# Layer-norm and weight-sum stage of a transformer block: loads of x on another queue, three buffers, and work spread over three engines

## The chip, the cores and the metric

The kernel runs on 8 cores of one Trainium2 chip. Each core takes one of the 8 sequences and runs the same program on it. The metric is the device time of the slowest core in microseconds (us), as a median over runs. Engines: TensorE (PE in the profile), VectorE (DVE), ScalarE (ACT), GpSimd (POOL), and SyncE (SP), which here only issues transfers.

## The reference, cut to what matters

```python
x = x + attn(layernorm(x), Wq, Wk, Wv, Wo)      # x: 8 x 4096 x 1024, f32; one head, d_k = 128, causal
x = x + ffn(layernorm(x), w_gate, w_up, w_down)  # 1024 -> 4096 -> 1024

def layernorm(x):                    # no gain, no bias
    return (x - mean(x)) / sqrt(var(x) + 1e-5)

def weight_quant(w):                 # one scale for a whole matrix
    scale = 1.0 / clip(mean(abs(w)), 1e-5)
    return clip(round(w * scale), -1, 1) / scale
# ffn: down(silu(gate(x)) * up(x)); every matmul takes weight_quant(w) and activations rounded to 8 bits a row
```

The scale of a weight matrix needs the sum of |w| over all of it, so each of the three matrices (16 MB each in f32) is read once for its sum and once more to be quantized.

## The kernel before

A core's 4096 rows of x are 32 tiles of 128 rows (`NT`). The program is written down engine by engine: `sc.op(engine, fn, waits, inc)` appends an instruction to the list of one engine ('t' TensorE, 'v' VectorE, 's' ScalarE, 'g' GpSimd, 'q' SyncE), with the semaphore values that it waits for. Each engine runs its list strictly in the order in which the calls were made, its transfers among it. An instruction whose wait is not met holds all that stands behind it on its engine. There is no scheduler: the order of the Python calls is the order of the work.

The stages are:

1. **Phase 1** (lines 162 to 307): for each of 32 tiles, load x, compute mean and variance, normalize, transpose, and compute Q, K and V. Between the tiles the weight matrices are read in 96 pieces of 128x1024 f32 (512 KB) and the sum of |w| of each piece goes to a column of `wsums`.
2. `emit_scales` (L309): three small serial chains from `wsums` to the scales of the three matrices.
3. Attention in eight groups of four tiles, with the second read and quantization of the weights between them (`emit_w2_piece`, L355).
4. Output projection and first residual, gate and up matmuls, down matmul. These take most of the time, and the change does not touch them.

The change is in phases 1 and 2 of this list. The loop of phase 1 (L294 to L302) is, for tile i: `emit_p1_A(i + 1)`, `emit_p1_B(i)`, `emit_p1_geo(i)`, then three calls of `emit_w1_piece`.

- `emit_xload_p1` (L164) loads tile i of x into one of two buffers, `x_st[i % 2]`. GpSimd issues it (L169), after the normalization of tile i-2 has read the buffer.
- `emit_p1_A(i)` (L217): the sum of x on VectorE (L222), the sum of squares on ScalarE (L227, Square with an accumulator).
- `emit_p1_B(i)` (L230): mean, its square and the variance on VectorE (L235, L237, L239, each behind a drain), the square root on ScalarE (L242), the reciprocal and the bias on VectorE (L244, L247), and then the normalization on ScalarE (L249), which writes `ln1_sb`, the first quarter of `nqh_sb`. Below it is called Ident(i).
- `emit_p1_geo(i)` (L257): 8 transposes on TensorE (L262), their eviction on VectorE (L265), 24 matmuls for Q, K and V (L271, L275, L279), then the evictions of Q and V on VectorE (L282, L286) and of K on ScalarE (L284).
- `emit_w1_piece(idx)` (L189): SyncE loads a piece into one of four staging buffers (L194) once the sum that read that buffer four pieces ago is done; ScalarE sums |w| (L198, Abs with an accumulator). The four buffers are the halves of `wst2` (named wstage in the profile) and parts of `nqh_sb` and `nqt_sb`.

So in phase 1 GpSimd's list holds only x loads, and SyncE's only loads of weight pieces.

## Time and profile before

| what | us |
|---|---|
| median of 2 runs | 2716.04 (2715.21 to 2716.87) |
| the profiled execution, its own time | 2719.91 |
| its span, slowest core (core 6) | 2718.4 |
| spans of the 8 cores | 2704.9 to 2718.4 |
| phase 1 on core 6, start to the last sum of a weight piece | about 393 |

The profiled execution took 2719.9 us, 1.5 us more than the span between the first and the last instruction of its slowest core, and 3.9 us more than the median of the runs. A row of the timeline has the start and the duration in us, the engine, the line of the kernel, the operation, what it writes and reads, a count, and in brackets how long its engine stood idle before it and what ended that. "SPq" is a transfer issued by SyncE. In the table of transfers the last number is the time from issue to landing.

### The profile page before, as it was taken

To read this page: it belongs to the slowest core of one execution; us is meant where nothing else is said; L and a number is where in the kernel's file an instruction comes from. 1 tells how busy PE (TensorE), PEld (TensorE's weight loads), DVE (VectorE), ACT (ScalarE), POOL (GpSimd) and SP (SyncE) were. 2 spreads that over 40 slices of the span, in tenths; PEclk is the share of its full clock that TensorE was granted. 3 is DMA by queue.
4 is the path that set the end of the run, shared out by engine and by line. 5 is a ranking of instruction groups with operands and counts; after the bars stand their busy time and mean duration, and the time that the engine had idled before them with its cause. 6 is when DMAs were issued, how large, how long until landed. Compare 5 with 4: busy or idle time off the path is not lost.

```text
span 2718.4 us, 25524 instructions; the slowest of 8 cores (2704.9 to 2718.4 us)
## 1 busy us (share of the span) xinstructions
PE 1694.8 (62%) x9479; PEld 881.5 (32%) x9618; DVE 912.9 (34%) x1481; ACT 862.2 (32%) x893; POOL 50.1 (2%) x104
## 2 busy tenths in 40 slices
PE   1333331222212377778778778778778766999999
PEld 1222231222200133333334334334334333444444
...
GB/s 151 188 183 184 186 168 263 218 95 102 102 199 268 124 24 47 32 39 47 31 39 47 32 39 47 31 39 47 31 39 47 16 74 205 155 155 155 154 150 115
DMA packets 74603, 290.09 MB, mean 107 GB/s; under 512 B 10864, under 2 KB 12912, under 8 KB 62192
## 3 DMA queue, kind: packets, MB, share of 16 engines
...
## 4 chain that ended last, share of the span: by engine, by line
PE 57%; DVE 11%; ACT 11%; DMA 10%; issue 8%; DVEq 2%; POOL 1%; ACTq 0%; POOLq 0%; SPq 0%
PE pb L760 18%; PE pb L753 17%; PE pb L899 16%; DMA wdqh<-wdq_st 5%; DVE h_sb L772 3%; DMA x_st<-x 3%; ACT kres L770 3%; ACT nqh_sb L249 1%; DVE st_cols L777 1%; ACT wdq_st L380 1%; PE pb L464 1%; ACT ln_scr L227 1%; PE pb L439 1%; ACT wstage L198 1%; DVEq L369 1%
## 5 line engine op out<-in xcount | busy, mean ns | idle before, releaser
L753 PE MATMUL pb<-wgq,qres 128*128 128x512 bf16 x1952 | 772.5, 396 | 254.1 <-DVE qres L736 251.3
L760 PE MATMUL pb<-wuq,qres 128*128 128x512 bf16 x2048 | 807.8, 394 | 43.0 <-DVE h_sb L772 38.1
L899 PE MATMUL pb<-wdq_sb,nqt_in 128*128 128x512 bf16 x2007 | 442.2, 380 | 24.8 <-DMA nqt_in<-nqh 22.4
L772 DVE SCALAR_TENSOR_TENSOR h_sb<-pb,st_cols,kres 128x1024 f32<-128x1024 f32 x128 | 164.3, 1284 | 739.0 <-ACT kres L770 739.0
L753 PEld LDWEIGHTS pb<-wgq,qres 128*128 128x128 bf16 x2048 | 207.3, 101 | 552.0 <-issue 333.7
L770 ACT ACTIVATE kres<-pb,st_cols 128x1024 f32<-128x1024 f32 x128 | 142.7, 1115 | 497.3 <-PE pb L760 335.2
L760 PEld LDWEIGHTS pb<-wuq,qres 128*128 128x128 bf16 x2048 | 206.0, 101 | 254.3 <-issue 35.5
L899 PEld LDWEIGHTS pb<-wdq_sb,nqt_in 128*128 128x128 bf16 x2048 | 200.9, 98 | 265.9 <-issue 25.7
L464 PE MATMUL pb<-qres,kres 128*128 128x128 bf16 x528 | 51.1, 255 | 242.1 <-ACT pt L482 227.7
L830 ACT ACTIVATE nqh_sb<-h_sb,konst 128x4096 bf16<-128x4096 f32 x32 | 118.6, 3708 | 215.0 <-DVE h_sb L828 215.0
L262 PE MATMUL pb<-ident_sb,nqh_sb 128*128 128x128 bf16 x256 | 32.4, 307 | 239.8 <-ACT nqh_sb L249 239.8
L909 DVE SCALAR_TENSOR_TENSOR out_sb<-pb,c_all,x_in 128x512 f32<-128x512 f32 x32 | 24.0, 751 | 431.1 <-PE pb L899 431.1
L777 DVE TENSOR_REDUCE st_cols<-h_sb 128x1 f32<-128x1024 f32 x128 | 156.1, 1220 | 11.7
L464 PEld LDWEIGHTS pb<-qres,kres 128*128 128x128 bf16 x528 | 40.8, 116 | 247.8 <-issue 245.0
L262 PEld LDWEIGHTS pb<-ident_sb,nqh_sb 128*128 128x128 bf16 x256 | 24.8, 138 | 247.1 <-issue 247.1
L828 DVE TENSOR_SCALAR h_sb<-h_sb,st_cols,konst 128x4096 f32<-128x4096 f32 x32 | 77.2, 2411 | 5.6 <-DVE c_all L826 5.6
L702 ACT ACTIVATE qres<-ln_scr,konst 128x1024 bf16<-128x1024 f32 x32 | 36.7, 1147 | 130.4 <-DVE ln_scr L695 130.4
L609 PE MATMUL pb<-wo_sb,ot_sb 128*128 128x512 bf16 x30 | 18.2, 607 | 88.1 <-DVE ot_sb L571 85.3
L802 ACT ACTIVATE nqt_sb<-pb 128x2048 bf16<-128x2048 bf16 x31 | 58.2, 1877 | 20.7 <-PE pb L795 20.7
L482 ACT ACTIVATE pt<-pb,konst 128x1024 bf16<-128x1024 f32 x56 | 59.2, 1118 | 9.8 <-PE pb L464 5.1
L795 PE MATMUL pb<-ident_sb,nqh_sb 128*128 128x128 bf16 x992 | 60.4, 219 | 0.0
L795 PEld LDWEIGHTS pb<-ident_sb,nqh_sb 128*128 128x128 bf16 x992 | 58.0, 98 | 7.3
...
## 6 DMA issues: line engine op xcount, KB each, us to landing
nqh<-nqt_sb ACTq DMA_DIRECT2D x32, 1024.0 KB, 3.9
nqt_in<-nqh SPq DMA_DIRECT2D x32, 1024.0 KB, 5.2
x_st<-x POOLq DMA_DIRECT2D x48, 512.0 KB, 4.9
x_st<-x1h SPq DMA_DIRECT2D x32, 512.0 KB, 3.3
x_in<-x1h SPq DMA_DIRECT2D x32, 512.0 KB, 6.8
y<-out_sb ACTq DMA_DIRECT2D x32, 512.0 KB, 6.9
wstage<-wdt SPq DMA_DIRECT2D x24, 512.0 KB, 4.4
wstage<-wgt SPq DMA_DIRECT2D x16, 512.0 KB, 5.5
```

Of the source, the lines that this page charges most:

```text
L464: tt = sc.op('t', (lambda k=k, q=q, pbst=pbst, off=off, j=j: (lambda e: e.matmul(pbst[:, off + j * 128: off + (j + 1) * 128], kres[:, k * ...
L482: s_exp_last[pp] = sc.op('s', (lambda pp=pp, ptx=ptx: (lambda e: e.activation(pt_row[ptx][:, 0:1024], pb[pp][:, 0:1024], AF.Exp, scale=sms ...
L753: tt = sc.op('t', (lambda c=c, o0=o0, gb=gb, half=half, par=par: (lambda e: e.matmul(gb[:, half * 512:(half + 1) * 512], xqTb[par][:, c * ...
L760: tt = sc.op('t', (lambda c=c, o0=o0, ub=ub, half=half, par=par: (lambda e: e.matmul(ub[:, half * 512:(half + 1) * 512], xqTb[par][:, c * ...
L770: s_silu_q[(i, qtr)] = sc.op('s', (lambda gb=gb, i=i: (lambda e: e.activation(g_s, gb, AF.Silu, scale=c1g_p[i % 2])))(), waits=sw, inc='S')
L772: v_stt_q[(i, qtr)] = sc.op('v', (lambda qtr=qtr, ub=ub, i=i: (lambda e: e.scalar_tensor_tensor(h_sb[:, qtr * 1024:(qtr + 1) * 1024], ub, ...
L777: sc.op('v', (lambda qtr=qtr: (lambda e: e.reduce_max(mh4[:, qtr:qtr + 1], h_sb[:, qtr * 1024:(qtr + 1) * 1024], axis=AX, apply_absolute_v ...
L795: tt2 = sc.op('t', (lambda c=c, pbx=pbx, coff=coff: (lambda e: e.transpose(pbx.bitcast(BF16)[:, coff:coff + 128], nqh_sb[:, c * 128:(c + 1 ...
L802: ss2 = sc.op('s', (lambda fg=fg: (lambda e: e.activation(nqt_sb[:, 0:2048], fg.bitcast(BF16)[:, 0:2048], AF.Identity)))(), waits=sw2, inc ...
L828: vv = sc.op('v', lambda e: e.tensor_scalar(h_sb, h_sb, s2q_c, cb_c, ALU.mult, ALU.add), waits=[('V', v_stt_q[(i, 3)])], inc='V')
L830: s_nqh_t[i] = sc.op('s', lambda e: e.activation(nqh_sb, h_sb, AF.Identity, bias=ng_c), waits=[('V', vv)], inc='S')
L899: tt = sc.op('t', (lambda c=c, half=half, par=par: (lambda e: e.matmul(dps[par][:, half * 512:(half + 1) * 512], nqt_in[par][:, c * 128:(c ...
```

## The change

The change rewrites phase 1, and nothing in the later stages but two lists of waits.

- x has three buffers: the two halves of `x2_st` and the first half of `wst2`. The loads are issued by SyncE instead of GpSimd, with three semaphores of their own, after Ident(i-3) and the sum of tile i-3.
- The weight pieces have three staging buffers instead of four. Of each two pieces one is summed by ScalarE as before and the next by VectorE (a reduction with absolute value).
- `emit_p1_A` runs two tiles ahead instead of one. `emit_p1_B` is split: `B1(i + 1)` computes mean and variance a tile ahead, `B2(i)` the rest. The mean, the variance and the bias are computed by GpSimd, the square of the mean and the reciprocal by VectorE. The drains between them are gone; waits on semaphores stand in their place.
- `emit_scales` waits for all of phase 1 on ScalarE before its first reduction, and no longer for a matrix's own sums alone.

```diff
-    w1stages = [wst2[:, 0:1024], wst2[:, 1024:2048],
+    w1stages = [wst2[:, 1024:2048],
                 nqh_sb.bitcast(F32)[:, 512:1536], nqt_sb.bitcast(F32)[:, 512:1536]]
...
     def emit_xload_p1(i):
-        par = i % 2
+        par = i % 3
         w = []
-        if i >= 2:
-            w.append(('S', s_lastx[i - 2]))
-        v = sc.op('g', (lambda i=i, par=par: (lambda e: e.dma_start(
-            out=x_st[par], in_=x_d[i * 128:(i + 1) * 128, :])))(), waits=w, inc='DGX%d' % par, n=16)
+        if i >= 3:
+            w += [('S', s_lastx[i - 3]), ('V', v_s1[i - 3])]
+        v = sc.op('q', (lambda i=i, par=par: (lambda e: e.dma_start(
+            out=x3[par], in_=x_d[i * 128:(i + 1) * 128, :])))(), waits=w, inc='DPX%d' % par, n=16)
...
     def emit_w1_piece(idx):
         wi, src, wid = wpieces[idx]
-        par = idx % 4
+        par = idx % 3
         dstap = w1stages[par][:, 0:wid]
-        w = [('S', s_abs[idx - 4])] if idx >= 4 else []
+        w = [s_abs[idx - 3]] if idx >= 3 else []
         v = sc.op('q', (lambda src=src, dstap=dstap: (lambda e: e.dma_start(out=dstap, in_=src)))(),
                   waits=w, inc='DQW%d' % par, n=16)
...
-        s_abs[idx] = sc.op('s', (lambda dstap=dstap, col=col: (lambda e: e.activation(
-            dstap, dstap, AF.Abs, accum_out=col)))(),
-            waits=[dq_p1w[idx]], inc='S')
+        if idx % 2 == 0:
+            s_abs[idx] = ('S', sc.op('s', (lambda dstap=dstap, col=col: (lambda e: e.activation(
+                dstap, dstap, AF.Abs, accum_out=col)))(),
+                waits=[dq_p1w[idx]], inc='S'))
+        else:
+            s_abs[idx] = ('V', sc.op('v', (lambda dstap=dstap, col=col: (lambda e: e.reduce_sum(
+                col, dstap, axis=AX, apply_absolute_value=True)))(),
+                waits=[dq_p1w[idx]], inc='V'))
...
+    def emit_p1_B1(i):
+        c = p1c[i % 3]
+        gw = [('V', v_s1[i])]
...
+        g_m[i] = sc.op('g', (lambda c=c: (lambda e: e.tensor_scalar(
+            c['m'], c['s1'], INV_D, None, ALU.mult)))(), waits=gw, inc='G')
...
+        v_m2[i] = sc.op('v', (lambda c=c: (lambda e: e.tensor_scalar(
+            c['m2'], c['s1'], INV_D, c['m'], ALU.mult, ALU.mult)))(), waits=vw, inc='V')
...
+        g_var[i] = sc.op('g', (lambda c=c: (lambda e: e.tensor_scalar(
+            c['var'], c['sq'], INV_D, c['m2'], ALU.mult, ALU.subtract)))(), waits=gw, inc='G')
+
+    def emit_p1_B2(i):
...
+        s_sd[i] = sc.op('s', (lambda c=c: (lambda e: e.activation(
+            c['sd'], c['var'], AF.Sqrt, bias=eps_c)))(), waits=sw, inc='S')
...
+        v_rstd[i] = sc.op('v', (lambda c=c: (lambda e: e.reciprocal(c['rstd'], c['sd'])))(),
+                          waits=vw, inc='V')
...
+        g_bm[i] = sc.op('g', (lambda c=c: (lambda e: e.tensor_scalar(
+            c['bm'], c['m'], -1.0, c['rstd'], ALU.mult, ALU.mult)))(), waits=gw, inc='G')
         s_ln1 = sc.op('s', (lambda xs=xs, c=c: (lambda e: e.activation(
             ln1_sb, xs, AF.Identity, scale=c['rstd'], bias=c['bm'])))(),
-            waits=[('V', vv)], inc='S')
+            waits=[('G', g_bm[i])], inc='S')
         s_lastx[i] = s_ln1
-        if i + 2 < NT:
-            emit_xload_p1(i + 2)
+        if i + 3 < NT:
+            emit_xload_p1(i + 3)
...
+    emit_p1_A(1)
+    emit_p1_B1(0)
     w1_next = 0
     for i in range(NT):
+        if i + 2 < NT:
+            emit_p1_A(i + 2)
         if i + 1 < NT:
-            emit_p1_A(i + 1)
-        s_ln1x = emit_p1_B(i)
+            emit_p1_B1(i + 1)
+        s_ln1x = emit_p1_B2(i)
...
-                tot_col, cols, axis=AX)))(), waits=[('S', wlast[wi])], inc='V')
+                tot_col, cols, axis=AX)))(), waits=[wlast[wi], s_abs[30 + 32 * wi], ('S', p1_S)], inc='V')
```

**The queue of SyncE.** Before, SyncE's list in the middle of phase 1 is weight pieces only, and each waits (on ScalarE's semaphore S) for the sum four pieces back. The x loads stand alone in GpSimd's list. First SyncE, from its start:

```order
L129 DMA ident_sb<-ident 128x128
L130 DMA mask_sb<-mask 128x128
L194 DMA wstage<-wgt 128x1024 x2
L194 DMA nqh_sb<-wgt 128x1024
L194 DMA nqt_sb<-wgt 128x1024
L194 DMA wstage<-wgt 128x1024 [waits S] x2
L194 DMA nqh_sb<-wgt 128x1024 [waits S]
```

The same stretch after the change, from the fourth tile of x on; x goes to `x_st` or to the first half of `wstage`, pieces to the second half, `nqh_sb` and `nqt_sb`:

```order
L171 DMA x_st<-x 128x1024 [waits S,V]
L196 DMA wstage<-wgt 128x1024
L196 DMA nqh_sb<-wgt 128x1024
L196 DMA nqt_sb<-wgt 128x1024
L171 DMA x_st<-x 128x1024 [waits S,V]
L196 DMA wstage<-wgt 128x1024
L196 DMA nqh_sb<-wgt 128x1024 [waits V]
L196 DMA nqt_sb<-wgt 128x1024
```

In front of each three pieces now stands a load of x, which waits for Ident three tiles before it, and the pieces behind it cannot be issued sooner. Pieces that show no wait on S have it covered by that of the x load.

**One tile on ScalarE.** Before, from one normalization (L249) to the next, where `DQW` are pieces and `DGX` x landing:

```order
L249 ACTIVATE nqh_sb<-x_st,st_cols 128x1024 [waits V]
L284 ACTIVATE kres<-pb 128x128 [waits T]
L198 ACTIVATE wstage,wsums<-wstage 128x1024 [waits DQW0]
L198 ACTIVATE wstage,wsums<-wstage 128x1024 [waits DQW1]
L198 ACTIVATE nqh_sb,wsums<-nqh_sb 128x1024 [waits DQW2]
L227 ACTIVATE ln_scr,st_cols<-x_st 128x1024 [waits DGX0,S]
L242 ACTIVATE st_cols<-st_cols,konst 128x1 [waits V]
```

After, a tile in which ScalarE has two of the three pieces (in the next it has one, and VectorE two); `DPX` is x landing, `G` GpSimd:

```order
L284 ACTIVATE nqh_sb<-wstage,st_cols 128x1024 [waits G]
L319 ACTIVATE kres<-pb 128x128 [waits T]
L201 ACTIVATE wstage,wsums<-wstage 128x1024 [waits DQW0]
L201 ACTIVATE nqt_sb,wsums<-nqt_sb 128x1024 [waits DQW2]
L244 ACTIVATE ln_scr,st_cols<-wstage 128x1024 [waits DPX2,S]
L272 ACTIVATE st_cols<-st_cols,konst 128x1 [waits V]
```

The order of the kinds is the same, with one sum less, and the Square (L244) is that of the tile after next.

**The same tile on VectorE** where VectorE has two pieces. Before:

```order
L286 CAST vres<-pb 128x128
L222 TENSOR_REDUCE st_cols<-x_st 128x1 [waits DGX1]
L235 TENSOR_SCALAR st_cols<-st_cols 128x1
L237 TENSOR_TENSOR st_cols<-st_cols 128x1
L239 TENSOR_SCALAR st_cols<-st_cols 128x1
L244 RECIPROCAL st_cols<-st_cols 128x1 [waits S]
L247 TENSOR_SCALAR st_cols<-st_cols 128x1
```

After:

```order
L321 CAST vres<-pb 128x128
L205 TENSOR_REDUCE wsums<-wstage 128x1 [waits DQW0]
L205 TENSOR_REDUCE wsums<-nqt_sb 128x1 [waits DQW2]
L237 TENSOR_REDUCE st_cols<-x_st 128x1 [waits DPX1]
L257 TENSOR_SCALAR st_cols<-st_cols 128x1 [waits G]
L277 RECIPROCAL st_cols<-st_cols 128x1 [waits S]
```

Two sums of weight pieces now stand ahead of the reciprocal on which the next normalization depends, and the bias behind it has gone to GpSimd.

## Rows read from the trace of the kernel before

**Rows 1.** The page, part 2: PE busy tenths in 40 slices of the span.

```profile
PE   1333331222212377778778778778778766999999
```

**Rows 2.** Waits of POOL and of SP's queue, 20 to 390 us: total, times, longest.

```profile
POOL x_st L169 <- ACT nqh_sb L249: 342.1, 30, 25.0
SPq L934 <- ACT wstage L198: 176.2, 46, 31.0
```

**Rows 3.** Timeline of one tile's cycle in phase 1.

```profile
201.57 1.24 ACT L249 ACTIVATE nqh_sb<-x_st,st_cols 128x1024 bf16<-128x1024 f32 x1 [0.67 <-DVE st_cols L247]
...
203.36 0.53 POOL L169 DMA_DIRECT2D x_st<-x  x1 [10.91 <-ACT nqh_sb L249]
...
207.72 0.28 ACT L284 ACTIVATE kres<-pb 128x128 bf16<-128x128 f32 x1 [4.91 <-PE pb L279]
...
207.89 1.05 ACT L198 ACTIVATE wstage<-wstage 128x1024 f32<-128x1024 f32 x1
...
208.40 1.22 DVE L222 TENSOR_REDUCE st_cols<-x_st 128x1 f32<-128x1024 f32 x1 [0.18 <-DMA x_st<-x]
...
209.97 1.04 ACT L198 ACTIVATE nqt_sb<-nqt_sb 128x1024 f32<-128x1024 f32 x1
...
211.01 1.04 ACT L227 ACTIVATE ln_scr<-x_st 128x1024 f32<-128x1024 f32 x1
...
212.05 0.28 ACT L242 ACTIVATE st_cols<-st_cols,konst 128x1 f32<-128x1 f32 x1
212.43 0.16 DVE L244 RECIPROCAL st_cols<-st_cols 128x1 f32<-128x1 f32 x1 [2.00 <-ACT st_cols L242]
...
213.00 1.24 ACT L249 ACTIVATE nqh_sb<-x_st,st_cols 128x1024 bf16<-128x1024 f32 x1 [0.67 <-DVE st_cols L247]
```

**Rows 4.** Timeline: first and last normalization of phase 1.

```profile
29.21 1.24 ACT L249 ACTIVATE nqh_sb<-x_st,st_cols 128x1024 bf16<-128x1024 f32 x1 [0.67 <-DVE st_cols L247]
...
383.74 1.24 ACT L249 ACTIVATE nqh_sb<-x_st,st_cols 128x1024 bf16<-128x1024 f32 x1 [0.67 <-DVE st_cols L247]
```

**Rows 5.** Windows, steady phase 1: each engine's busy us (x), PEclk, DMA share, GB/s.

```profile
200.00:300.00 100.00, 33.56 (x288) 29.28 (x288) 28.14 (x78) 49.76 (x94) 4.76 (x9) 0.55 0.66 188
```

**Rows 6.** Timeline: four x tiles issued in a row by POOL, and their landing.

```profile
778.56 1.12 POOL L415 DMA_DIRECT2D x_st<-x  x2 [41.08 <-DMA wdqh<-wdq_st]
...
779.66 1.05 POOL L415 DMA_DIRECT2D wstage<-x  x2
```

**Rows 7.** Transfers issued 779.6 to 779.7 us, then 780.1 to 780.6: us to landing.

```profile
wstage<-x POOLq DMA_DIRECT2D x1, 512.0 KB, 7.1
...
wstage<-x POOLq DMA_DIRECT2D x2, 512.0 KB, 7.5
```

**Rows 8.** Timeline: first two 1 MB loads of the second weight read; landing of the second.

```profile
393.46 0.33 SPq L364 DMA_DIRECT2D x_st<-wgt  x1
...
393.84 0.43 SPq L364 DMA_DIRECT2D wstage<-wgt  x1
```

**Rows 9.** Transfers issued 393.8 to 393.9 us: us to landing.

```profile
wstage<-wgt SPq DMA_DIRECT2D x1, 1024.0 KB, 10.2
```

**Rows 10.** The page, part 6: the quickest 512 KB load.

```profile
x_st<-x1h SPq DMA_DIRECT2D x32, 512.0 KB, 3.3
```

**Rows 11.** GpSimd's mask multiply, by its line: ns min/median/max.

```profile
L489 POOL TENSOR_TENSOR pt<-pt,mask_sb x32: 416/426/428, 402.1 to 737.1; 128x128 bf16<-128x128 bf16 x32
```

**Rows 12.** Timeline of the start: third SyncE load of 512 KB, and x landing.

```profile
2.92 0.43 SPq L194 DMA_DIRECT2D nqh_sb<-wgt  x1
...
24.64 1.28 ACT L227 ACT_TABLE_LOAD   x1 [24.64 <-DMA x_st<-x]
```

**Rows 13.** Transfers issued in the first 25 us: us to landing.

```profile
nqh_sb<-wgt SPq DMA_DIRECT2D x1, 512.0 KB, 11.2
```

**Rows 14.** Timeline behind the last tile: first scale reduction, first attention matmul.

```profile
390.35 0.19 DVE L316 TENSOR_REDUCE st_cols<-wsums 128x1 f32<-128x32 f32 x1
...
398.41 1.23 PE L464 MATMUL pb<-qres,kres 128*128 128x128 bf16 x10 [0.47 <-DVE wscales L335]
```

More of the change, by code:

```diff
@@ L84, in _build @@
     x_st = [x2_st[:, 0:D], x2_st[:, D:2 * D]]
+    x3 = None
     ln_scr = sb("ln_scr", [128, D], F32)
@@ L207, in _build @@
     v_evQ = [0, 0]; s_evK = [0, 0]; v_evV = [0, 0]
-    p1c = [
-        dict(s1=st[:, 0:1], sq=st[:, 1:2], m=st[:, 2:3], m2=st[:, 3:4],
-             var=st[:, 4:5], sd=st[:, 5:6], rstd=st[:, 6:7], bm=st[:, 7:8]),
-        dict(s1=st[:, 8:9], sq=st[:, 9:10], m=st[:, 10:11], m2=st[:, 11:12],
-             var=st[:, 12:13], sd=st[:, 13:14], rstd=st[:, 14:15], bm=st[:, 15:16]),
-    ]
-    s_sqa = [0] * NT
+    p1c = [dict(s1=st[:, 8 * k + 0:8 * k + 1], sq=st[:, 8 * k + 1:8 * k + 2],
+                m=st[:, 8 * k + 2:8 * k + 3], m2=st[:, 8 * k + 3:8 * k + 4],
+                var=st[:, 8 * k + 4:8 * k + 5], sd=st[:, 8 * k + 5:8 * k + 6],
+                rstd=st[:, 8 * k + 6:8 * k + 7], bm=st[:, 8 * k + 7:8 * k + 8])
+           for k in range(3)]
+    s_sqa = [0] * NT
+    v_s1 = [0] * NT
+    g_m = [0] * NT
+    v_m2 = [0] * NT
+    g_var = [0] * NT
+    s_sd = [0] * NT
+    v_rstd = [0] * NT
+    g_bm = [0] * NT
     def emit_p1_A(i):
-        par = i % 2
-        xs = x_st[par]
+        par = i % 3
+        xs = x3[par]
         c = p1c[par]
-        sc.op('v', lambda e: e.drain())
-        sc.op('v', (lambda xs=xs, c=c: (lambda e: e.reduce_sum(c['s1'], xs, axis=AX)))(),
-              waits=[dg_x[i]], inc='V')
+        vw = [dg_x[i]]
+        if i >= 3:
+            vw.append(('G', g_m[i - 3]))
+        v_s1[i] = sc.op('v', (lambda xs=xs, c=c: (lambda e: e.reduce_sum(c['s1'], xs, axis=AX)))(),
+                        waits=vw, inc='V')
         sw = [dg_x[i]]
@@ L226, in emit_p1_A @@
             sw.append(('S', s_sqa[i - 1]))
+        if i >= 3:
+            sw.append(('G', g_var[i - 3]))
         s_sqa[i] = sc.op('s', (lambda xs=xs, c=c: (lambda e: e.activation(
             ln_scr, xs, AF.Square, accum_out=c['sq'])))(), waits=sw, inc='S')
[L230 to L248 removed]
@@ new lines, in emit_p1_B1 @@
+    def emit_p1_B1(i):
+        c = p1c[i % 3]
+        gw = [('V', v_s1[i])]
+        if i >= 3:
+            gw.append(('V', v_m2[i - 3]))
+        g_m[i] = sc.op('g', (lambda c=c: (lambda e: e.tensor_scalar(
+            c['m'], c['s1'], INV_D, None, ALU.mult)))(), waits=gw, inc='G')
+        vw = [('G', g_m[i])]
+        if i >= 3:
+            vw.append(('G', g_var[i - 3]))
+        v_m2[i] = sc.op('v', (lambda c=c: (lambda e: e.tensor_scalar(
+            c['m2'], c['s1'], INV_D, c['m'], ALU.mult, ALU.mult)))(), waits=vw, inc='V')
+        gw = [('V', v_m2[i]), ('S', s_sqa[i])]
+        if i >= 3:
+            gw.append(('S', s_sd[i - 3]))
+        g_var[i] = sc.op('g', (lambda c=c: (lambda e: e.tensor_scalar(
+            c['var'], c['sq'], INV_D, c['m2'], ALU.mult, ALU.subtract)))(), waits=gw, inc='G')
@@ new lines, in emit_p1_B2 @@
+    def emit_p1_B2(i):
+        par = i % 3
+        xs = x3[par]
+        c = p1c[par]
+        sw = [('G', g_var[i])]
+        if i >= 3:
+            sw.append(('V', v_rstd[i - 3]))
+        s_sd[i] = sc.op('s', (lambda c=c: (lambda e: e.activation(
+            c['sd'], c['var'], AF.Sqrt, bias=eps_c)))(), waits=sw, inc='S')
+        vw = [('S', s_sd[i])]
+        if i >= 3:
+            vw += [('G', g_bm[i - 3]), ('S', s_lastx[i - 3])]
+        v_rstd[i] = sc.op('v', (lambda c=c: (lambda e: e.reciprocal(c['rstd'], c['sd'])))(),
+                          waits=vw, inc='V')
+        gw = [('V', v_rstd[i])]
+        if i >= 3:
+            gw.append(('S', s_lastx[i - 3]))
+        g_bm[i] = sc.op('g', (lambda c=c: (lambda e: e.tensor_scalar(
+            c['bm'], c['m'], -1.0, c['rstd'], ALU.mult, ALU.mult)))(), waits=gw, inc='G')
```

28 lines of the change are left out of this document (6 added, 22 removed).

## The prediction

> **What bounds the kernel now.** I read the busy tenths first [rows 1]. A slice is 68 us, so phase 1 is the first six of 40, and TensorE works there at 1 to 3 tenths: phase 1 is not bound by matmuls. In steady phase 1 ScalarE is busy 49.8 us of 100, VectorE 28.1 and the transfer engines 0.66 of the time at 188 GB/s [rows 5]. No engine is full, so a chain with a round trip bounds it. The timeline of one tile shows that chain [rows 3]. Ident starts at 201.57 and ends at 202.81. K's eviction starts at 207.72, after 4.91 us in which ScalarE waits for transposes, an eviction and 24 matmuls. Three sums of weight pieces and the Square follow 1.04 us apart, to 212.05, then the root, the reciprocal and the bias, and the next Ident at 213.00. One cycle is 11.43 us, and the first and the last Ident confirm it over 31 cycles: (383.74 - 29.21) / 31 = 11.44 [rows 4].
>
> The reader is to see what does not set this cycle. The load of x is issued at 203.36, 0.55 us after Ident's end, and the tile is there by 208.40, when VectorE reduces it; ScalarE wants it only at 211.01 [rows 3]. The weight pieces run ahead, four deep, on SyncE's queue, which waits only for free buffers [rows 2]. GpSimd's 342 us of waiting for Ident [rows 2] hold nothing behind them but the next x load. The transfers of a tile, four times 512 KB, are thus spread over the cycle and hidden behind the matmuls and the sums.
>
> **What the change does to that.** The list of SyncE decides. A load of x waits for Ident(i), and the three pieces of that tile stand behind it. Their buffers are free before Ident(i), since their sums stand ahead of it. So all four transfers, 2.1 MB, are issued together, right after Ident(i). The next Ident stands behind all four on every path: ScalarE's list has the sum and the Square ahead of the root, VectorE's list has its sums and the reduction of x ahead of the reciprocal. The third buffer of x and the A two tiles ahead don't help: x(i+3) is still issued after Ident(i) and read before Ident(i+1). A cycle becomes issue, landing of all four, then the rest of the chain.
>
> **Landing of the four, L.** The trace has no such burst in phase 1, so I bound it.
> - Nearest row: GpSimd issues four x tiles of the same size at 778.56 and 779.66, two each [rows 6]. The third lands after 7.1 us; the last two have a median of 7.5, so the fourth takes 7.9 [rows 7]. With its issue at about 780.19 it lands at 788.1, 9.5 us after the first issue.
> - From above: two loads of 1 MB on SyncE, issued at 393.46 and 393.84, of which the second takes 10.2 [rows 8, 9]: 10.6 us for the same bytes, with all cores loading.
> - From below, in this phase: transfers are at work 0.66 of 11.43 = 7.5 us a cycle [rows 5], 1.9 a tile. The quickest 512 KB load takes 3.3 [rows 10], so 1.4 are fixed, and L = 1.4 + 7.5 = 8.9. If of those 3.3 us 1.9 were fixed and only 1.4 spent moving, and the burst moved at that rate, L would be 1.9 + 4 x 1.4 = 7.5.
>
> I take 9.4, just under the first. The ends are 7.5 and 10.6.
>
> The page "DMA: Bandwidth & Descriptors" of the Trainium skill, in its "Anatomy of one DMA", fits a transfer as about 2.0 us plus bytes at 436 GB/s. By it L would be an estimated 6.8 and the cycle 11.5, which is no change. The rows speak against it: 2.1 MB took 9.5 and 10.6 us [rows 6 to 9].
>
> **The rest of the chain.** Where ScalarE has the last piece: its sum and the Square to the root's end, 212.33 - 209.97 = 2.36; the reciprocal to its end, 0.26; the bias, now on GpSimd; Ident, 1.24 [rows 3]. The bias before cost 0.41 (from 212.59 to 213.00). GpSimd's only computing row is a 128x128 multiply at 0.43 us [rows 11], and it began its x issue 0.55 us after its releaser [rows 3]. So the bias costs between 0.3 (less than before, as a drain goes) and 1.1 (0.43 + 0.55 and the hop back); I take 0.7, between them. With 0.1 for SyncE's first issue (at most GpSimd's 0.55):
> 0.1 + 9.4 + 2.36 + 0.26 + 0.7 + 1.24 = 14.06 us.
> Where VectorE has the last piece, its sum and the reduction of x, 1.22 each [rows 3], with the square of the mean, about 0.2, give 2.6 in place of 2.36: the same cycle within 0.3. I use 14.06, 2.63 more than 11.43.
>
> What is hidden: one and a half sums leave ScalarE a tile (1.6 us), and mean, variance and drains leave VectorE; both now fall into time in which the engines wait for the landing, and are worth nothing. GpSimd's mean and variance run a tile ahead, behind the same landing; if that cover went they would cost one or two GpSimd operations, 0.4 to 1 us. The matmuls of a tile (4.91 + 0.28 us) end before the first piece lands, and are off the path.
>
> **The start.** Before, x(0) lands at 24.64 behind the projection weights on GpSimd's queue, and Ident(0) ends at 30.45 [rows 4, 12]. Now three x tiles head SyncE's queue. The third load of 512 KB there was issued at 2.92 and took 11.2 us [rows 12, 13], so x(2) lands at 14.1. Its Square (1.04), the root (0.28), reciprocal and bias (1.0) and Ident (1.24) follow: Ident(0) ends at about 17.6, 13 us sooner. Its first matmuls wait for the projection weights, but the burst behind Ident(0) lands later still.
>
> **The end.** The last x load is issued after Ident(28). The pieces behind it wait only for buffers, so two cycles have no burst in the chain: 4.91 + 0.28 for the matmuls, one or two sums (2.4 on VectorE), root, reciprocal, bias and Ident (2.5): 10.0 each, 1.4 less than 11.43. After the last Ident, at 384.98 before, attention began at 398.41 [rows 4, 14], 13.4 later; its scale chain began at 390.35, beside the last sums, and took 8.0. Now the chain waits for all sums: 5.4 to the end of V's eviction (K's starts at 4.91), 2.4 for VectorE's two, 8.0: 15.8, which is 2.4 more.
>
> **The sum.** 29 cycles x 2.63 = +76.3; two at -1.4 = -2.9; start -13.0; end +2.4: +62.8 us. Stages behind attention are untouched. The profiled execution took 2719.9, 3.9 above the median of the runs shown; with +62.8 it would be 2782.7, and the median 2716.0 becomes 2778.8. I take 2779. About 2% (54 us) is what a measurement of this kernel can tell from no change; it corresponds to a cycle of 13.8 us, so the forecast lies just beyond it.
>
> **The rivals.**
> - *The burst is quick.* The four tiles land in 7.5 us, at the rate of a lone load. For it: the cores' mean traffic falls with a longer cycle, and one queue is left in place of two. Against it: both bursts in the trace. Cycle 12.2: 29 x 0.8 = 23, less 13.5 of start and end, +9: 2725, or anything up to 2765 for L between. By the skill's fit above the loads would be all but hidden, and the sum 29 x 0.03 - 13.5 = -13, or 2703.
> - *The loads don't bind, and the kernel gets faster.* One mechanism: the last tile lands before ScalarE has done with K's eviction and its first sum, 5.2 + 1.0 us behind Ident. Then the matmul chain sets the cycle as before, with 1.5 sums less and 0.3 more for GpSimd: 11.43 - 1.6 + 0.3 = 10.1, and 29 x -1.3 - 13.5 = -51: 2665. It needs L under about 6.1. For it: single x loads of 5 us in phase 1 [rows 3]. Against it: those have a quarter of the bytes.
> - *GpSimd is dear.* Its small operations cost 1.5 us rather than 0.7 with their hops, and the variance stands ahead of the bias in its list. Cycle 14.9 to 15.3: +87 to +98, some 2810. For it: 0.55 us to begin an issue. Against it: 0.43 us for a much larger operand [rows 11].
>
> **How the numbers follow.** Forecast 0.50, quick burst 0.34, loads not binding 0.05, GpSimd dear 0.11. Slower by over 2%: 0.44 of the forecast's 0.50 and all of the last, 0.55. Faster by over 2%: half of the second rival, 0.03. Within 2%: 0.42. The low end, L of 7.9, is 2735; I take 2730 for some of the quick bursts. The high end, L of 10.4, is 2716 + 29 x 3.6 - 13.5 = 2807; with part of a dearer GpSimd, 2815. The low end leaves 0.1 below it and the high end about 0.05 above.
>
> **What would show it.** Right: transfers from SyncE in groups of four right behind Ident, each cycle 13.5 to 14.5 us; ScalarE's idle time in phase 1 ended by landing pieces, not by K's matmuls; DMA share about 0.55 at 150 GB/s; the first Ident near 16; the last near 444; the later stages as long as before. Wrong: ScalarE's waits still ended by the matmuls for K; pieces issued before Ident ends; the fourth tile landing under 8 us behind it; a gap of over 1 us between reciprocal and Ident; or a difference of more than 5 us in the stages behind attention.

## The result, and the profile after

The median is 2753.1 us over 7 runs, beside 2717.6 us over 6 runs of the kernel before: the ratio is 1.0131, with a 95% interval of 1.0117 to 1.0145. The change makes the kernel 35.5 us slower. That is less than the 62.8 us forecast and inside the stated range of 2730 to 2815; by the bound of 2% it counts as no change, though the interval is clear of 1. Now and then an execution of any of these kernels is several per cent slower than the rest; ratios leave such executions out, and where they have moved a median, as in e3 (2821) and e9 (2804), the text goes by the ratio or by an undisturbed execution. The profiled execution took 2751.7 us, its slowest core (core 6, as before) 2750.1.

The first view is the table of waits of SyncE's queue, 40 to 400 us, which answers to [rows 2]:

```profile
SPq L974 <- ACT nqh_sb L284: 306.7, 27, 12.5
```

Before, SyncE waited for sums of pieces; now all of its waiting, 306.7 us, is for Ident. The steady stretch, with the columns of [rows 5]:

```profile
200.00:300.00 100.00, 27.70 (x239) 24.10 (x237) 34.13 (x58) 33.60 (x61) 5.06 (x22) 0.53 0.48 166
```

The transfer engines are busy 0.48 of the time in place of 0.66, ScalarE 33.6 us in place of 49.8, and VectorE 34.1 in place of 28.1. ScalarE and the transfer engines stand idle for longer, VectorE has taken over sums and is still idle for two thirds of the time, and the tile takes longer: the chain has grown, not the work. The timeline answers to [rows 3]. Its first four rows are of a tile in which VectorE has two of the three pieces; from 209.05 on it is a tile in which ScalarE has two:

```profile
195.53 1.24 ACT L284 ACTIVATE nqh_sb<-x_st,st_cols 128x1024 bf16<-128x1024 f32 x1 [0.79 <-POOL st_cols L282]
...
196.85 0.33 SPq L171 DMA_DIRECT2D x_st<-x  x1
...
205.72 1.22 DVE L205 TENSOR_REDUCE wsums<-nqt_sb 128x1 f32<-128x1024 f32 x1 [1.38 <-DMA nqt_sb<-wut]
...
208.42 0.29 POOL L262 TENSOR_SCALAR st_cols<-st_cols 128x1 f32<-128x1 f32 x1 [12.81 <-DVE st_cols L277]
...
209.05 1.24 ACT L284 ACTIVATE nqh_sb<-wstage,st_cols 128x1024 bf16<-128x1024 f32 x1 [2.22 <-POOL st_cols L282]
210.36 0.33 SPq L171 DMA_DIRECT2D wstage<-x  x1
...
210.78 0.39 SPq L196 DMA_DIRECT2D wstage<-wut  x1
211.21 0.42 SPq L196 DMA_DIRECT2D nqh_sb<-wut  x1
...
211.73 0.39 SPq L196 DMA_DIRECT2D nqt_sb<-wut  x1
...
215.21 0.28 ACT L319 ACTIVATE kres<-pb 128x128 bf16<-128x128 f32 x1 [4.92 <-PE pb L314]
...
216.12 1.06 ACT L201 ACTIVATE wstage<-wstage 128x1024 f32<-128x1024 f32 x1 [0.64 <-DMA wstage<-wut]
...
218.73 1.06 ACT L201 ACTIVATE nqt_sb<-nqt_sb 128x1024 f32<-128x1024 f32 x1 [1.46 <-DMA nqt_sb<-wut]
...
219.78 1.04 ACT L244 ACTIVATE ln_scr<-wstage 128x1024 f32<-128x1024 f32 x1
...
220.82 0.28 ACT L272 ACTIVATE st_cols<-st_cols,konst 128x1 f32<-128x1 f32 x1
221.20 0.16 DVE L277 RECIPROCAL st_cols<-st_cols 128x1 f32<-128x1 f32 x1 [1.24 <-ACT st_cols L272]
221.54 0.26 POOL L282 TENSOR_SCALAR st_cols<-st_cols 128x1 f32<-128x1 f32 x1 [1.04 <-DVE st_cols L277]
...
221.90 1.24 ACT L284 ACTIVATE nqh_sb<-x_st,st_cols 128x1024 bf16<-128x1024 f32 x1 [0.79 <-POOL st_cols L282]
```

In the second tile Ident ends at 210.29. SyncE issues x at 210.36, 0.07 us later, and the three pieces by 211.73. K's eviction comes at 215.21, as ever 4.9 us behind Ident, and then ScalarE waits for a piece (to 216.12), and again for the last one (to 218.73). From there sum, Square, root, reciprocal, bias and Ident follow, each as soon as the one before it is done. The landing times behind this, in the table of transfers from 200 to 300 us:

```profile
wstage<-wut SPq DMA_DIRECT2D x7, 512.0 KB, 5.3
nqh_sb<-wut SPq DMA_DIRECT2D x7, 512.0 KB, 6.2
nqt_sb<-wut SPq DMA_DIRECT2D x7, 512.0 KB, 6.9
x_st<-x SPq DMA_DIRECT2D x4, 512.0 KB, 4.0
wstage<-x SPq DMA_DIRECT2D x3, 512.0 KB, 3.9
```

x takes 4.0, the pieces behind it 5.3, 6.2 and 6.9 us: they land in the order of the queue. The last is issued 1.4 us behind x, so by these medians the four land in about 8.3 us. From one issue of x to the landing of the last piece the single tiles on core 6, from Ident(3) to Ident(27), take 7.4 to 9.6 us, 8.6 on the mean: 8.2 where ScalarE has two pieces, 8.9 where VectorE has two, as in the first tile above (196.85 to 205.72).

The start, and the end of phase 1:

```profile
7.43 1.28 ACT L244 ACT_TABLE_LOAD   x1 [7.43 <-DMA x_st<-x]
...
12.92 1.06 ACT L244 ACTIVATE ln_scr<-x_st 128x1024 f32<-128x1024 f32 x1 [3.05 <-DMA x_st<-x]
...
17.43 1.06 ACT L244 ACTIVATE ln_scr<-wstage 128x1024 f32<-128x1024 f32 x1 [3.36 <-DMA wstage<-x]
...
19.58 1.24 ACT L284 ACTIVATE nqh_sb<-x_st,st_cols 128x1024 bf16<-128x1024 f32 x1 [0.81 <-POOL st_cols L282]
```

```profile
404.78 1.24 ACT L284 ACTIVATE nqh_sb<-wstage,st_cols 128x1024 bf16<-128x1024 f32 x1 [0.79 <-POOL st_cols L282]
...
424.50 1.24 ACT L284 ACTIVATE nqh_sb<-x_st,st_cols 128x1024 bf16<-128x1024 f32 x1 [0.80 <-POOL st_cols L282]
...
433.36 0.19 DVE L356 TENSOR_REDUCE st_cols<-wsums 128x1 f32<-128x32 f32 x1
...
441.44 1.23 PE L504 MATMUL pb<-qres,kres 128*128 128x128 bf16 x10 [0.47 <-DVE wscales L375]
```

x(0), x(1) and x(2) land at 7.4, 12.9 and 17.4 us, and Ident(0) begins at 19.58 where it began at 29.21 [rows 4]. Ident(29) begins at 404.78, Ident(31) at 424.50, and attention at 441.44 in place of 398.41 [rows 14], 43.0 us later. The span grew by 31.7 only. Where the 43.0 come from and where 11 of them go, on core 6 (us):

| term | forecast | measured | from |
|---|---|---|---|
| 29 cycles | 29 x +2.63 = +76.3 | +53.6 | (404.78 - 19.58) / 29 = 13.28 a cycle, before 11.44 |
| last two cycles | -2.9 | -3.2 | (424.50 - 404.78) / 2 = 9.86 |
| start | -13.0 | -9.6 | Ident(0) begins 19.58, before 29.21 |
| behind the last Ident | +2.4 | +2.3 | 441.44 - 425.74 = 15.7, before 13.4 |
| attention and second weight read | 0 | -3.7 | 376.4, before 380.1 |
| later stages | 0 | -7.5 | 1932.3, before 1939.8 |

Core 6 alone is a poor measure of the last two rows. The table below gives for each kernel of this study the cycle (first to last Ident, over 31), the first attention matmul and the length of the attention stage (from there to the first transpose of the output projection), as the mean of all 8 cores, and the spread of that first matmul over the cores.

| kernel | cycle | first attention matmul | spread | attention stage |
|---|---|---|---|---|
| before | 11.44 | 398.5 | 1.4 | 378.5 |
| changed | 12.97 | 437.4 | 11.6 | 370.5 |
| e1_pieces_first | 10.87 | 372.0 | 3.1 | 372.3 |
| e2_x_on_gpsimd | 10.70 | 378.4 | 3.9 | 373.2 |
| e3_sums_on_act | 13.03 | 439.0 | 14.3 | 369.0 |
| e4_half_pieces | 10.90 | 373.3 | 6.3 | 370.9 |
| e5_before_x_on_sp | 12.80 | 426.6 | 12.6 | 370.8 |
| e6_before_late_scales | 11.44 | 401.8 | 2.3 | 377.9 |
| e7_pf_early_scales | 10.85 | 372.1 | 4.3 | 371.4 |
| e8_sums_under_matmuls | 8.21 | 284.9 | 13.4 | 369.6 |
| e9_before_drift | 11.44 | 442.9 | 3.7 | 374.9 |
| e10_reorder_only | 12.62 | 421.3 | 11.8 | 370.3 |
| e11_before_drift32 | 11.44 | 565.9 | 5.0 | 374.7 |

On the mean of the cores phase 1 and the scale chain are 38.9 us longer, the attention stage 8.0 shorter and the rest 1.7 shorter: +29.2, and the mean of the spans grew by 29.4. The slowest core grew by 31.7: the spans of the cores now lie 19 us apart, before 13.5.

### The profile page after: what moved, and what is told of

The parts are those of the page before. It is cut to its first block, busy times and chain, and to the rows that moved or that the text cites. A ratio compares the mean times of both kernels' runs of the same rounds, so it can differ in the third digit from the quotient of the medians.

```text
span 2750.1 us, 25407 instructions; the slowest of 8 cores (2731.1 to 2750.1 us)
## 1 busy us (share of the span) xinstructions
PE 1693.5 (62%) x9479; PEld 882.9 (32%) x9618; DVE 946.5 (34%) x1433; ACT 817.2 (30%) x797; POOL 56.2 (2%) x168
## 4 chain that ended last, share of the span: by engine, by line
PE 54%; DMA 16%; DVE 10%; ACT 8%; issue 8%; DVEq 2%; SPq 1%; POOL 1%; ACTq 0%; POOLq 0%
PE pb L800 18%; PE pb L793 17%; PE pb L939 16%; DMA wdqh<-wdq_st 4%; DMA nqt_sb<-wgt 3%; DVE h_sb L812 3%; ACT kres L810 3%; DMA nqt_sb<-wut 2%; DMA nqt_sb<-wdt 2%; ACT nqh_sb L284 1%; DVE st_cols L817 1%; ACT wdq_st L420 1%; PE pb L504 1%; PE pb L479 1%; DMA wstage<-x 1%
## 5 line engine op out<-in xcount | busy, mean ns | idle before, releaser
L817 DVE TENSOR_REDUCE st_cols<-h_sb 128x1 f32<-128x1024 f32 x128 | 156.1, 1220 | 12.8 <-issue 1.3
```

What stands on the lines that cost most here:

```text
L817: sc.op('v', (lambda qtr=qtr: (lambda e: e.reduce_max(mh4[:, qtr:qtr + 1], h_sb[:, qtr * 1024:(qtr + 1) * 1024], axis=AX, apply_absolute_v ...
```

## The experiments

**e1_pieces_first: the place in SyncE's list.** The piece loads stand ahead of the load of x.

```diff
+        for k in range(3):
+            emit_w1_load(w1_next + k)      # the three loads of emit_w1_piece, its sums stay where they are
         s_ln1x = emit_p1_B2(i)             # Ident(i), then the load of x(i+3)
```

> The changed kernel with one difference: on SyncE's list the three piece loads of tile i stand ahead of the load of x(i+3), not behind it. Theory (the wait of the x load for Ident holds the pieces back, so four loads land in one burst inside the chain; measured cycle 13.3 us): pieces are issued as their buffers come free, 1 to 4 us before Ident ends, only x is issued behind Ident, the matmul chain and two sums at most set the cycle: 10.2 to 10.8 us, the last Ident 75 to 95 us sooner than in the changed kernel, total 2665 to 2690. Rival (the transfers themselves, 2.1 MB a tile, are too slow with three buffers, whatever the order): cycle stays 12.5 to 13.5 and the total within 10 us of 2753. It also tells a second thing: in the changed kernel the stage between the first attention matmul and the output projection is 8 us shorter than before, on every core. If that comes from cores that have drifted apart and collide less in the second weight read, it should go back to 376 to 382 us when phase 1 runs in step again; if from the longer head start of the loads over attention (7.8 us against 5.0), it should stay at 366 to 376.

Measured: 2685.8 us, ratio to the kernel before 0.9885 (0.9867 to 0.9903), cycle 10.87. The changed kernel minus one ordering is not slower than before but 32 us faster, 67 below the changed one. The cycle came out 0.1 above the expected range, and the cores did not quite run in step again (spread 3.1 us); the attention stage stayed at 372.3, where the head start theory had it. Its timeline (core 5) shows what is left:

```profile
208.67 0.33 SPq L171 DMA_DIRECT2D wstage<-x  x1
...
213.52 0.28 ACT L326 ACTIVATE kres<-pb 128x128 bf16<-128x128 f32 x1 [4.92 <-PE pb L321]
...
213.69 1.05 ACT L208 ACTIVATE nqh_sb<-nqh_sb 128x1024 f32<-128x1024 f32 x1
...
215.06 1.21 DVE L212 TENSOR_REDUCE wsums<-nqt_sb 128x1 f32<-128x1024 f32 x1
215.21 0.33 SPq L196 DMA_DIRECT2D wstage<-wut  x1
215.63 0.38 SPq L196 DMA_DIRECT2D nqh_sb<-wut  x1
215.82 1.06 ACT L251 ACTIVATE ln_scr<-wstage 128x1024 f32<-128x1024 f32 x1 [0.99 <-DMA wstage<-x]
...
216.34 0.33 SPq L196 DMA_DIRECT2D nqt_sb<-wut  x1
...
217.43 0.15 DVE L284 RECIPROCAL st_cols<-st_cols 128x1 f32<-128x1 f32 x1
...
218.37 1.24 ACT L291 ACTIVATE nqh_sb<-x_st,st_cols 128x1024 bf16<-128x1024 f32 x1 [1.22 <-POOL st_cols L289]
```

The pieces are issued at 215.21 to 216.34, as the sums of the pieces before them end, and the load of x alone stands behind Ident (208.67). K's eviction is followed at once by a sum (213.69): the pieces are there. In this tile, where VectorE has two sums, they and the reduction of x fill VectorE from 213.93 on and the reciprocal comes at 217.43, behind them, though ScalarE had finished the root. So the odd tiles are now bound by VectorE's list, at 11.0 us, and most of the even ones, at 10.5, by the matmul chain.

**e2_x_on_gpsimd: the same from the other side.** The changed kernel with the x loads on GpSimd, as before.

```diff
-        v = sc.op('q', (lambda i=i, par=par: (lambda e: e.dma_start(
+        v = sc.op('g', (lambda i=i, par=par: (lambda e: e.dma_start(
             out=x3[par], in_=x_d[i * 128:(i + 1) * 128, :])))(), waits=w, inc='DPX%d' % par, n=16)
```

> The changed kernel with x loads issued by GpSimd again, behind the bias in its list; all else as changed. Theory (head of line on SyncE): pieces no longer wait for Ident, cycle 10.2 to 11.0 us, total 2670 to 2700; the start is later again, since x(0) to x(2) are queued behind the projection weights (Ident(0) at 25 to 31 us in place of 19.6). Rival (three staging buffers in place of four, or the small operations on GpSimd, are what costs): cycle 12.5 or more, total 2750 or above.

Measured: 2693.7 us, ratio 0.9918 (0.9902 to 0.9934), cycle 10.70, Ident(0) at 27.4 to 31.1 us over the cores. Three stages, sums on two engines and small operations on GpSimd are all still there, and the kernel is 24 us faster than before. The start that SyncE's queue had won is given back: Ident(0) begins 11.5 us later than in e1 on the mean of the cores, 31 cycles win 5.3 back, and attention begins 6.4 later, which is most of the 8 us by which e2 is behind e1.

**e3_sums_on_act: are the sums that were moved worth anything?** All three sums of a tile on ScalarE.

```diff
-        if idx % 2 == 0:
+        if True:
             s_abs[idx] = ('S', sc.op('s', (lambda dstap=dstap, col=col: (lambda e: e.activation(
```

> The changed kernel with all three sums of a tile on ScalarE; all else as changed. Theory (the chain is issue, landing of the last piece, one sum, Square, root, reciprocal, bias, Ident; the other sums fall into the landing): cycle 12.9 to 13.5 us, total within 10 us of 2753. Rival (ScalarE's own work counts, so that moving half of the sums is worth 1.5 x 1.04 us a tile): cycle 14.5 to 15, total 2795 to 2805.

Measured: ratio 1.0149 (1.0127 to 1.0170), some 2758 us; cycle 13.03 where the changed kernel has 12.97. Its windows (100 to 250 us, core 1), with ScalarE at 71 us of 150 against 50.6 on core 6 of the changed kernel:

```profile
100.00:250.00 150.00, 41.03 (x352) 35.80 (x352) 28.65 (x67) 70.98 (x127) 8.48 (x35) 0.55 0.45 154
```

```profile
100.00:250.00 150.00, 41.02 (x352) 35.78 (x352) 48.45 (x85) 50.62 (x90) 8.62 (x36) 0.51 0.45 154
```

40% more work for ScalarE, and the same transfer share, 0.45, and the same 352 matmuls in the window: it all fell into the wait for the landing, as the prediction had it.

**e4_half_pieces: bytes or latency?** The changed kernel with half of each piece loaded in phase 1; the other half of the buffers is zero, so the scales come from half of the weights.

```diff
+        src = src[:, 0:512]
...
-        v = sc.op('q', (lambda src=src, dstap=dstap: (lambda e: e.dma_start(out=dstap, in_=src)))(),
+        v = sc.op('q', (lambda src=src, dstap=dstap: (lambda e: e.dma_start(out=dstap[:, 0:512], in_=src)))(),
```

> The changed kernel with half of each weight piece loaded in phase 1 (512 of 1024 columns; the other half of each buffer is set to zero once), so the scales are computed from half of the weights. Sums keep their length. Theory (transfer time of the burst is in the chain): 0.79 of 2.1 MB less, so about 2.8 us less landing, until the matmul chain takes over at 10.2: cycle 10.4 to 10.9 us. Rival (a fixed latency of four transfers on one queue, not bytes, is what is waited for): cycle 12.5 or more.

Measured, in one run: 2688.4 us, cycle 10.90. The transfers, from 100 to 250 us:

```profile
nqt_sb<-wut SPq DMA_DIRECT2D x11, 256.0 KB, 5.1
...
wstage<-wut SPq DMA_DIRECT2D x10, 256.0 KB, 4.6
nqh_sb<-wut SPq DMA_DIRECT2D x10, 256.0 KB, 4.8
```

The last piece takes 5.1 us in place of 6.9 from its issue, and 2.1 us leave the cycle for 0.79 MB less. Bytes in the chain, as the theory says; a bare latency would have left the cycle at 13. The cycle is that of e1 (10.87), so it is the engines' own lists that bind again, and the run gives no finer price of a byte than that.

**e5_before_x_on_sp: one part of the change alone.** The kernel before, with the x loads in SyncE's list and nothing else.

```diff
-        v = sc.op('g', (lambda i=i, par=par: (lambda e: e.dma_start(
-            out=x_st[par], in_=x_d[i * 128:(i + 1) * 128, :])))(), waits=w, inc='DGX%d' % par, n=16)
+        v = sc.op('q', (lambda i=i, par=par: (lambda e: e.dma_start(
+            out=x_st[par], in_=x_d[i * 128:(i + 1) * 128, :])))(), waits=w, inc='DPX%d' % par, n=16)
```

> The kernel before with one part of the change alone: x loads are issued by SyncE in front of the three pieces of the tile, everything else (two x buffers, four stages, all sums on ScalarE, small operations on VectorE) as before. Theory (the place in SyncE's list is what costs): the pieces of tile i are issued behind Ident(i); three of four landings stand in the chain, but one stage of four is free earlier only in name, since the x load in front holds it. Landing 8.7 us, then one sum, Square, root, reciprocal, bias, Ident as in the changed kernel: cycle 12.8 to 13.6 us, start 8 to 12 us sooner, total 2745 to 2775. Rival (fourth stage and VectorE's spare time keep it hidden; the changed kernel is slow for its three stages or its operations on GpSimd): cycle 11.4 to 11.8, total 2705 to 2725.

Measured: 2743.7 us, ratio 1.0088 (1.0066 to 1.0110), cycle 12.80. This one edit brings 1.36 of the 1.53 us by which a cycle of the changed kernel is longer. The total is 1 us under the expected range; Ident(0) begins at 13.6 to 17.4 us, over 11 us sooner on every core and 14 on the mean, where 8 to 12 were expected.

**e6_before_late_scales and e7_pf_early_scales: the scale chain.** The kernel before with the wait for all of phase 1, and e1 without it:

```diff
-                tot_col, cols, axis=AX)))(), waits=[('S', wlast[wi])], inc='V')
+                tot_col, cols, axis=AX)))(), waits=[('S', wlast[wi]), ('S', p1_S)], inc='V')
```

```diff
-                tot_col, cols, axis=AX)))(), waits=[wlast[wi], s_abs[30 + 32 * wi], ('S', p1_S)], inc='V')
+                tot_col, cols, axis=AX)))(), waits=[wlast[wi], s_abs[30 + 32 * wi]], inc='V')
```

> The kernel before with the changed kernel's wait in the scale chain alone: its first reduction waits for all of phase 1 on ScalarE. The first attention matmul should come 2 to 3.5 us later. If the head start of the second weight read over attention is what shortened the attention stage (378.5 to 370.5 us on the mean of the cores), that stage gets shorter here by about the delay, and the total stays within 2 us of 2717. If drifted cores are what shortened it, the stage stays at 377 to 380 and the total is 2 to 4 us longer.

> The kernel with piece loads first (2685.8 us), with the scale chain waiting only for a matrix's own sums, as before the change. The third matrix still waits for the last sums, the first two do not: the first attention matmul comes 1 to 5 us sooner. Head start theory: the attention stage gets longer by the same, total within 2 us of 2686. Drift theory: attention stage unchanged at 372, total 2681 to 2685.

Measured: e6 has its first attention matmul 3.3 us later and an attention stage of 377.9, 0.6 shorter; its ratio of 0.9988 (0.9955 to 1.0021) does not tell 3 us from nothing. So the head start theory of the shorter attention stage falls. The head start is the time from the first load of the second weight read to the first attention matmul: 5.0 us before, 7.8 in the changed kernel, 8.0 in e6. e5 says the same from the other side: its head start is still 5.0 at most, and its stage takes 370.8. e7 says nothing: 2688.5 us, ratio 0.9869 (0.9813 to 0.9925), and the first attention matmul did not move (372.1 against 372.0). In these kernels VectorE's own list has the last sums of phase 1 ahead of the first reduction (which starts at 433.36 in the changed kernel, as the last of them ends), so the wait that was taken away was not the last one.

**e8_sums_under_matmuls: what the idle time is worth.** e1 with the loop in another order.

```diff
+        for k in range(3):
+            emit_w1_load(w1_next + k)
+        s_ln1x = emit_p1_B2b(i)               # Ident(i), load of x(i+3)
+        t_qkv = emit_p1_geo(i, s_ln1x)        # transposes, their eviction, matmuls
+        if i + 1 < NT:
+            emit_p1_B1(i + 1)
+        for _ in range(3):
+            if w1_next < len(wpieces):
+                emit_w1_piece(w1_next)        # the sums
+                w1_next += 1
         if i + 2 < NT:
             emit_p1_A(i + 2)
         if i + 1 < NT:
-            emit_p1_B1(i + 1)
+            emit_p1_B2a(i + 1)                # root, reciprocal, bias
+        emit_p1_geo2(i, t_qkv)                # evictions of Q, K, V
```

> The kernel with piece loads first, and the loop in another order: behind Ident(i) and its matmuls stand the sums of the pieces, Square and sum of tile i+2 and root, reciprocal and bias of tile i+1, and only then the evictions of Q, K and V of tile i. So the work that stood behind the 4.9 us wait for the matmuls goes into it. Theory (the chain Ident to matmuls to K's eviction is 1.24 + 4.9 + 0.3 = 6.5 us, the transfers 7.5 us a tile): cycle 7.8 to 8.8 us, bound by transfers, total 2600 to 2635. Rival (x(i+3) issued behind Ident(i) and needed by the Square in front of Ident(i+1) keeps a landing of 4 to 5 us plus Square, root and bias in the chain): cycle 8.9 to 9.8, total 2635 to 2665.

Measured: 2600.3 us, ratio 0.9567 (0.9499 to 0.9635), cycle 8.21. This version beats both kernels, by 118 and 153 us. One tile of it, and its windows (100 to 250 us, core 1):

```profile
156.67 1.24 ACT L294 ACTIVATE nqh_sb<-x_st,st_cols 128x1024 bf16<-128x1024 f32 x1 [0.86 <-POOL st_cols L287]
...
158.05 1.01 PE L307 MATMUL pb<-ident_sb,nqh_sb 128*128 128x128 bf16 x8 [2.62 <-ACT nqh_sb L294]
...
160.43 1.06 ACT L208 ACTIVATE wstage<-wstage 128x1024 f32<-128x1024 f32 x1 [2.52 <-DMA wstage<-wut]
...
163.03 1.06 ACT L208 ACTIVATE nqt_sb<-nqt_sb 128x1024 f32<-128x1024 f32 x1 [1.45 <-DMA nqt_sb<-wut]
...
164.08 1.04 ACT L251 ACTIVATE ln_scr<-x_st 128x1024 f32<-128x1024 f32 x1
...
165.12 0.28 ACT L277 ACTIVATE st_cols<-st_cols,konst 128x1 f32<-128x1 f32 x1
165.31 0.25 ACT L333 ACTIVATE kres<-pb 128x128 bf16<-128x128 f32 x1
...
166.19 1.24 ACT L294 ACTIVATE nqh_sb<-wstage,st_cols 128x1024 bf16<-128x1024 f32 x1 [0.63 <-POOL st_cols L287]
```

```profile
100.00:250.00 150.00, 67.27 (x584) 58.65 (x584) 76.80 (x139) 83.38 (x152) 13.60 (x56) 0.57 0.83 262
```

Between Ident (ends 157.91) and K's eviction (165.31) ScalarE now does its sums, the Square and the root. It waits 2.52 us for a piece before the first sum, and the transfer engines are busy 0.83 of the time at 262 GB/s where in the changed kernel they had 0.45 and 154 on core 6: the stage is close to bound by transfers.

**e10_reorder_only: the new order without the new queue.** e8 with the x load ahead of the pieces on SyncE again.

```diff
-        for k in range(3):
-            emit_w1_load(w1_next + k)
         s_ln1x = emit_p1_B2b(i)
```

> The kernel with sums under the matmuls (2600.3 us), but with SyncE's list as in the changed kernel again: the x load in front of the three pieces. Theory (the burst behind Ident is what binds, whatever the engines do meanwhile): ScalarE's pieces land 6 to 8.4 us behind Ident, then sum, Square, root, reciprocal, bias and Ident: cycle 12.4 to 13.3 us, total 2735 to 2760, so the new order alone is worth under 15 us against 2753. Rival (the new order by itself gives most of the 150 us): cycle under 10.5, total under 2690.

Measured: 2741.8 us, ratio 1.0078 (1.0038 to 1.0118), cycle 12.62. ScalarE's waits from 100 to 250 us, in which it does some twelve tiles:

```profile
ACT nqh_sb L208 <- DMA nqh_sb<-wut: 22.0, 3, 8.2
ACT nqh_sb L208 <- DMA nqh_sb<-wgt: 16.9, 2, 9.5
ACT wstage L208 <- DMA wstage<-wut: 16.6, 3, 5.6
ACT wstage L208 <- DMA wstage<-wgt: 16.6, 3, 5.6
```

It waits 5.6 us for the first piece in tiles with two of them, and 7 to 8.5 on the mean in tiles with one. So the order of the engines' work is worth 11 us with the burst in the chain and 85 without it (2685.8 to 2600.3). The gains of the two edits do not add up (67 and 11 us alone, 153 together): the queue decides what the order can give.

**e9_before_drift and e11_before_drift32: why is attention shorter?** The kernel before, with 8 and with 32 extra loads of 1 MB in a chain behind phase 1, whose data nothing uses; all that follows waits for the last.

```diff
+    for k in range(8):
+        w = [('S', p1_S), ('V', p1_V)] if k == 0 else [('DRX', drx)]
+        drx = sc.op('q', (lambda k=k: (lambda e: e.dma_start(
+            out=x2_st, in_=wgt_d[k * 128:(k + 1) * 128, 0:2048])))(), waits=w, inc='DRX', n=16)
```

> The kernel before with eight extra loads of 1 MB, one after another, behind phase 1 (work thrown away); attention's scale chain and the second weight read wait for the last. It tells whether drift of the cores alone shortens the attention stage. In the kernel before, the first attention matmuls of the 8 cores lie 1.4 us apart and the stage takes 378.5 us on the mean of the cores; in six other kernels they lie 3 to 15 us apart and it takes 369 to 373. Each extra load costs 5 to 6 us, so total 2757 to 2768 if nothing is given back. Drift theory: the loads are bound by transfers and spread the cores by more than 3 us, the stage takes 369 to 374, and the total is 4 to 9 us shorter than the loads' own time. Rival (something else in phase 1's end state makes it shorter): stage 377 to 380 in spite of a spread over 3 us. If the spread stays under 3 us the run tells nothing.

> The kernel before with 32 extra loads of 1 MB in a chain behind phase 1 (work thrown away), where the run with eight gave a spread of 3.7 us between the cores' first attention matmuls and an attention stage of 374.9 us, in between. Only the spread and the length of the attention stage count here, the total is some 165 us longer by the loads. Drift theory: spread 6 us or more, attention stage 368 to 372 us on the mean of the cores, as in the kernels with a spread of 7 to 15. Rival (the shorter stage comes from something else in how phase 1 ends): stage 376 to 380 at that spread. If the spread stays below 5 us it tells no more than the run with eight.

Measured: spreads of 3.7 and 5.0 us and stages of 374.9 and 374.7, each between the two expectations. The total of e9 is 2759.9, which is what its later start of attention (+44.4) and its shorter stage (-3.6) make of 2718. That of e11, one run, is 2884, to which its +167.4 and -3.8 come as well. So beyond the shorter stage the totals tell nothing. In the run with 32 loads the cores fall in two groups: 0, 3, 4 and 7 reach attention at 563 to 565.4 us and take 370 to 373 there, the others at 566 to 568 and take 377.5 to 379. Both runs have a head start of 8.1 us, as e6 has with 377.9 us for the stage, so the head start is not what shortens theirs. So part of the 8 us goes with the cores' drifting apart, but a spread of 5 us did not bring all of it, while e1 has 372.3 at a spread of 3.1. What the rest is stays open, and that collisions between cores are the cause was not shown.

## Why the prediction was right, and where its terms were off

- **The mechanism holds.** Four transfers in one burst behind Ident, with the next Ident behind all four. The waits of SyncE and the timeline show it, e1 and e2 remove it from either side and the cycle falls to 10.9 and 10.7, and e5 brings it into the kernel before. It was shown, not only argued.
- **The landing was over-estimated.** The step that failed is "I take 9.4, just under the first": the four landed in 8.6 us on the mean of core 6's tiles, 8.4 in the one shown from 209.05 on (210.36 to 218.73). With that 8.4 the chain comes to 13.1, and that tile took 12.9 (209.05 to 221.90); the tile before it, with two sums on VectorE, had a landing of 8.9 and took 13.5 (195.53 to 209.05). The mean on core 6 is 13.28 where the forecast had 14.06, and that 0.8 is the 0.8 of the landing. It made the sum 22.7 us too high. The bound from this phase was worked out from the transfer share of the kernel before, 0.66 of 11.43 = 7.5 us of work for 2.1 MB. In the changed kernel the same bytes need 0.46 of 12.97 = 6.0 us (mean of the cores). What I kept as an argument for the rival of the quick burst, that traffic gets lighter, pointed the right way, but it is not all of it: e1 and e2 carry more traffic than the kernel before and need 6.6 and 6.4 us. The truth lies between the forecast (9.4) and that rival (7.5). The result of 2753 us lies in the stretch that the prediction gave to the rival, "2725, or anything up to 2765 for L between", as much as in its own.
- **Slower by over 2%** had a chance of 0.55, and did not come true: 1.3%. The stated range held because it was wide. Of its signs, the groups of four right behind Ident came as written; the cycle on the mean of the cores (12.97), the transfer share on core 6 (0.48 at 166 GB/s, for 0.55 at 150), the first Ident (19.6 for 16) and the last (424.5 for 444) did not.
- **Two kinds of tile.** The same cycle "within 0.3" was forecast for both. On the mean of the cores they took 12.8 us (ScalarE has two pieces) and 13.55 (VectorE has two); 0.6 of the difference is the landing, 8.2 and 8.8. Why it differs was not isolated.
- **By the page "DMA: Bandwidth & Descriptors" of the Trainium skill** ("Anatomy of one DMA", 2.0 us plus bytes at 436 GB/s) the burst would have landed in an estimated 6.8 us, and the kernel would have been no slower. The page gives this fit for one transfer issued by GpSimd; taking four transfers of SyncE as one was my own step. The trace disagrees with that estimate: 8.6 us on the mean. What in the chip makes the difference, no run here isolates.
- **Bias on GpSimd.** From the reciprocal's end to Ident 0.54 us (221.36 to 221.90), forecast 0.7; its operation takes 0.26. In the tiles with two pieces on VectorE it is 0.79 us, since there the variance of the next tile stands ahead of the bias in GpSimd's list (the row at 208.42), as the rival of a dear GpSimd had it. At a quarter of a us in every second tile that rival is out all the same.
- **Start.** Forecast -13.0, measured -9.6: x(2) landed at 17.4, not 14.1. I had taken the third SyncE load of the kernel before on one core. On the 8 cores that load landed at 13.7 to 15.5 us, and x(2), in the same place of the list and issued at the same time, at 13.3 to 17.8; GpSimd's projection weights are on their way beside both. What makes the difference was not isolated. On the mean of the cores Ident(0) begins 10.9 us sooner.
- **End.** -2.9 and +2.4 came out as -3.2 and +2.3.
- **What is hidden.** Sums moved to VectorE worth nothing: right (e3, 0.06 us a cycle). But K's eviction still has ScalarE's longest single wait, 4.9 us a tile, and the landing only waits of 0.3 to 3.3 us behind it; my sign of error "ScalarE's waits still ended by the matmuls for K" was badly chosen, since the landing needs only to end the last wait.
- **"Stages behind attention are untouched"** held for those on the mean of the cores (-1.7 us); on core 6 they are 7.5 us shorter, which by itself would be a sign of error. The attention stage itself, of which I had not spoken, gave back 8.0 us.
